# FFN of layer 1: the last 48 rows of up share a weight tile with the last 48 rows of gate

## What is computed

```python
def _ghost_linear(x, idx, lut):
    w = lut[idx]
    return jnp.einsum('bsh,oh->bso', x, w)
gate = _ghost_linear(x, gate_idx, lut)     # gate_idx: 688 x 256
up = _ghost_linear(x, up_idx, lut)         # up_idx:   688 x 256
h = jax.nn.silu(gate) * up
return _ghost_linear(h, down_idx, lut)     # down_idx: 256 x 688
...
h = _layernorm(x, axis=-1) * (1 + cb) + sb
x = x + gb * _L1_ffn_ref(h, ...)
```

## Time and profile before

| what | value |
|---|---|
| median of 3 runs | 1310.63 us (1310.13 to 1314.87) |
| the profiled execution | 1310.77 us |
| its span, first to last instruction | 1309.0 us |
| mean granted TensorE clock | 0.971 of full speed |
| PE busy | 1192.1 us (91%) |
| DVE busy | 935.0 us (71%) |
| ACT busy | 686.7 us (52%) |
| POOL busy | 681.0 us (52%) |
| FFN of layer 1 | 1194.85 to 1309.0, 114 us |

### The profile page before, as it was taken

How to read it: one execution, slowest core, us unless ns; L and a number is a source line. 1 busy time by engine, 2 the same in 40 slices (tenths; PEclk the granted TensorE clock), 3 DMA queues, 4 the chain that set the end, 5 groups by cost and what they waited for, 6 DMA issues and landing times.

```text
span 1309.0 us, 22523 instructions
## 1 busy us (share of the span) xinstructions
PE 1192.1 (91%) x6940; PEld 870.5 (67%) x6940; DVE 935.0 (71%) x2757; ACT 686.7 (52%) x1599; POOL 681.0 (52%) x679
## 2 busy tenths in 40 slices
PE   6888897988569999999999999999999999999998
PEld 5445464545447677686786777867767777667787
DVE  5767787775567786877867868778778687676553
ACT  3356646564354645546546455465465564654432
POOL 0340101011135799998579999857999999000000
PEclk9789999999779999999999999999999999999999
DMA  6431012000124210320420302132022000000000
GB/s 219 132 80 50 26 50 89 26 34 1 65 85 125 76 38 0 135 70 30 139 95 5 129 7 70 49 121 92 26 111 69 2 33 32 0 2 1 17 17 33
DMA packets 36102, 77.93 MB, mean 60 GB/s; under 512 B 8152, under 2 KB 22336, under 8 KB 35248
## 3 DMA queue, kind: packets, MB, share of 16 engines
q1 hardware_dynamic: 26736, 47.13, 10.8%
q0 software_dynamic: 8128, 25.49, 6.0%
q10 hardware_dynamic: 1152, 4.19, 0.8%
HBM read 54.62 MB, written 22.04 MB: 59 GB/s over the span
## 4 chain that ended last, share of the span: by engine, by line
PE 37%; DVE 25%; issue 8%; ACT 3%; DVEq 0%; ACTq 0%
PE bank L1494 10%; PE bank L1468 7%; DVE qk L1093 6%; DVE qkst L1069 5%; PE bank L1479 5%; PE bank L297 5%; PE bank L299 5%; PE bank L298 5%; DVE negmax L1164 2%; DVE probs L1159 2%; DVE x L1149 2%; DVE ytmps L1146 1%; DVE sm L131 1%; DVE sm L129 1%; PE bank L1455 1%
## 5 line engine op out<-in xcount | busy, mean ns | idle before, releaser
L711 POOL TENSOR_SCALAR gtmp<-gidx,lut 128x344 f32<-128x344 int32 (+2 forms) x210 | 299.5, 1426 | 21.3
L1468 PE MATMUL bank<-kT,qT 128*128 128x128 f32 (+3 forms) x512 | 181.7, 444 | 13.2 <-ACT probs L887 13.1
L714 POOL TENSOR_TENSOR gacc<-gacc,gtmp 128x344 f32<-128x344 f32 (+2 forms) x210 | 183.6, 874 | 17.5
L887 ACT ACTIVATE probs<-bank,negmax 128x128 f32<-128x128 f32 (+3 forms) x256 | 135.1, 528 | 60.6 <-DVE negmax L1164 57.0
L297 PE MATMUL bank<-wgH,hL 128*128 128x512 f32 x384 | 155.3, 404 | 1.1 <-issue 1.1
L1164 DVE TENSOR_REDUCE negmax<-bank 128x1 f32<-128x128 f32 (+3 forms) x256 | 122.6, 483 | 42.4 <-PE bank L1469 40.5
L298 PE MATMUL bank<-wgL,hH 128*128 128x512 f32 x384 | 152.3, 397 | 0.0
L299 PE MATMUL bank<-wgH,hH 128*128 128x512 f32 x384 | 152.1, 396 | 0.0
L1494 PE MATMUL bank<-pT,v 128*128 128x512 f32 (+3 forms) x512 | 149.2, 434 | 0.8 <-ACT pT L879 0.7
L1103 DVE TENSOR_REDUCE negmax<-bank 128x1 f32<-128x512 f32 (+3 forms) x176 | 108.1, 636 | 57.4 <-PE bank L1398 57.0
L1069 DVE BATCH_NORM_STATS2 qkst<-qk 128x6 f32<-128x128 f32 x512 | 109.4, 280 | 46.4 <-issue 46.4
(11 more groups left out here) (221 smaller groups left out, 2682.4 us busy)
## 6 DMA issues: line engine op xcount, KB each, us to landing
hH<-h_saved SPq DMA_DIRECT2D x16, 512.0 KB, 4.0
hL<-h_saved SPq DMA_DIRECT2D x16, 512.0 KB, 4.9
qst<-q_parts SPq DMA_DIRECT2D x96, 64.0 KB, 2.4
w_saved<-shi POOLq DMA_DIRECT2D x24, 256.0 KB, 2.3
w_saved<-slo POOLq DMA_DIRECT2D x24, 256.0 KB, 2.6
sraw<-in_wqkv POOLq DMA_DIRECT2D x18, 256.0 KB, 3.0
wgH<-w_saved SPq DMA_DIRECT2D x3, 1536.0 KB, 8.4
wgL<-w_saved SPq DMA_DIRECT2D x3, 1536.0 KB, 11.6
```

The costliest lines, as they stand in the source:

```text
L711: link(pool.tensor_scalar(tmp if j else acc, part, float(j), lut1[0:rows, j:j + 1], ALU.is_equal, ALU.mult))
L714: link(pool.tensor_tensor(acc, acc, tmp, ALU.add))
L1468: pe.matmul(bank[SCORE_BANKS[i % 3]][:, 0:n], qT[:, h, t * P:n], kT[:, h, 0:n], start=True, stop=False)
```

## The change

Gate and up now lie in one row of columns: `wguH` and `wguL` are [128, 2, 11 x 128]. Up's five full tiles come first, then from `GATE0 = 640` on gate's five, and the eleventh tile holds the last 48 rows of gate in its columns 0 to 47 and the last 48 of up in its columns 64 to 111, with zeros between. So the step m = 5 has one product of 6 matmuls in place of two, into `bank[2]`: gate comes out on partitions 0 to 63 and up on 64 to 127. ACT reads the silu's input at partitions 0 to 63 and writes it to `sg` at 64 to 127, DVE multiplies there and writes `hf` at 0 to 63. The following steps of m = 5, `hmH`, `hmL` and the down matmuls, use 64 partitions. Two of POOL's jobs write their result in two pieces, and POOL waits for its own memsets before the first job.

```diff
-        wguH = sb(s1, "wguH", [P, 2, KT, MT * P], F32R)
-        wguL = sb(s1, "wguL", [P, 2, KT, MT * P], F32R)
+        wguH = sb(s1, "wguH", [P, KT, (2 * MT - 1) * P], F32R)
+        wguL = sb(s1, "wguL", [P, KT, (2 * MT - 1) * P], F32R)
...
+            def places(w, k, o):
+                if w == "gate":
+                    return [(slice(0, PIECE), k, GATE0 + o)]
+                if o == 0:
+                    return [(slice(0, PIECE), k, 0)]
+                full = INTER - LAST - o
+                return [(slice(0, full), k, o), (slice(full, PIECE), k, GATE0 + (MT - 1) * P + UP)]
...
+            pool.memset(f32(wguH[:, :, GATE0 + INTER:]), 0.0).then_inc(f_zero, 1)
+            pool.memset(f32(wguL[:, :, GATE0 + INTER:]), 0.0).then_inc(f_zero, 1)
+            pool.wait_ge(f_zero, 2)
             pool.wait_ge(loaded_lut, 16)
...
-                pool.tensor_copy(hi, gacc[:, 0:cols]).then_inc(f_hi, 1)
-                pool.wait_ge(f_hi, i + 1)
-                pool.tensor_tensor(lo, gacc[:, 0:cols], f32(hi), ALU.subtract).then_inc(f_lo, 1)
+                for c, hi, lo in to:
+                    pool.tensor_copy(hi, gacc[:, c]).then_inc(f_hi, 1)
+                pool.wait_ge(f_hi, pieces[i + 1])
+                for c, hi, lo in to:
+                    pool.tensor_tensor(lo, gacc[:, c], f32(hi), ALU.subtract).then_inc(f_lo, 1)
...
-                    act.activation(sg[:, m % 2, :], bank[2 * (m % 2)][:, :], ACT.Silu).then_inc(f_silu, 1)
+                    rows, to = (slice(0, P),) * 2 if m < MT - 1 else (slice(0, UP), slice(UP, P))
+                    act.activation(sg[to, m % 2, :], bank[2 * (m % 2)][rows, :], ACT.Silu).then_inc(f_silu, 1)
                     act.wait_ge(f_h, b * MT + m + 1)
                     act.wait_ge(y2_pe, b * 2)
-                    act.activation(hmH[:, m, :], hf[:, m % 2, :], ACT.Copy).then_inc(f_hhi, 1)
+                    act.activation(hmH[rows, m, :], hf[rows, m % 2, :], ACT.Copy).then_inc(f_hhi, 1)
...
-                    dve.tensor_tensor(hf[:, m % 2, :], bank[2 * (m % 2) + 1][:, :], sg[:, m % 2, :], ALU.mult).then_inc(f_h, 1)
+                    if m < MT - 1:
+                        rows = slice(0, P)
+                        dve.tensor_tensor(hf[:, m % 2, :], bank[2 * (m % 2) + 1][:, :], sg[:, m % 2, :], ALU.mult).then_inc(f_h, 1)
+                    else:
+                        rows = slice(0, UP)
+                        dve.tensor_tensor(hf[rows, m % 2, :], bank[2 * (m % 2)][UP:P, :], sg[UP:P, m % 2, :], ALU.mult).then_inc(f_h, 1)
...
-                    for w in range(2):
+                    for w, first in enumerate((GATE0, 0) if m < MT - 1 else (GATE0,)):
+                        cols = slice(first + m * P, first + (m + 1) * P)
                         for k in range(KT):
-                            last = mm3(pe, bank[2 * (m % 2) + w][:, :], wguH[:, w, k, m * P:(m + 1) * P],
-                                       wguL[:, w, k, m * P:(m + 1) * P], hH[:, k, :], hL[:, k, :], k == 0, k == KT - 1)
+                            last = mm3(pe, bank[2 * (m % 2) + w][:, :], wguH[:, k, cols],
+                                       wguL[:, k, cols], hH[:, k, :], hL[:, k, :], k == 0, k == KT - 1)
...
-                        last = mm3(pe, bank[4 + t // 2][:, (t % 2) * D:(t % 2 + 1) * D], hmH[:, m, rows], hmL[:, m, rows],
-                                   wdH[:, m, :], wdL[:, m, :], m == 0, m == MT - 1)
+                        ks = slice(0, P if m < MT - 1 else UP)
+                        last = mm3(pe, bank[4 + t // 2][:, (t % 2) * D:(t % 2 + 1) * D], hmH[ks, m, rows], hmL[ks, m, rows],
+                                   wdH[ks, m, :], wdL[ks, m, :], m == 0, m == MT - 1)
```

More of the change, by code:

```diff
@@ L42 @@
 LAST = INTER - (MT - 1) * P
+UP = P // 2
 LUT = 16
 PIECE = INTER // 2
+GATE0 = (MT - 1) * P
 NMOD = 6
@@ L682, in _ @@
             pool.dma_start(lut1[:, :], a["lut"].to_broadcast([P, LUT])).then_inc(loaded_lut, 16)
[L684 to L687, removed]
+            def places(w, k, o):
[5 more added lines that the diff above has]
+                return [(slice(0, full), k, o), (slice(full, PIECE), k, GATE0 + (MT - 1) * P + UP)]
+            jobs = [(a[f"idx_{w}"][k * P:(k + 1) * P, o:o + PIECE], P, PIECE,
+                     [(c, wguH[:, kk, to:to + c.stop - c.start], wguL[:, kk, to:to + c.stop - c.start]) for c, kk, to in places(w, k, o)])
+                    for w in ("gate", "up") for k in range(KT) for o in range(0, INTER, PIECE)]
+            jobs += [(a["idx_down"][m * P:min((m + 1) * P, INTER), :], min(P, INTER - m * P), D,
+                      [(slice(0, D), wdH[:, m, :], wdL[:, m, :])]) for m in range(MT)]
+            pieces = [sum(len(job[3]) for job in jobs[:i]) for i in range(len(jobs) + 1)]
             def load_job(i):
-                src, rows, cols, hi, lo = jobs[i]
+                src, rows, cols, _ = jobs[i]
                 pool.dma_start(gidx[0:rows, i % 2, 0:cols], src).then_inc(loaded_idx[i % 2], 16)
@@ L696, in _ @@
             load_job(0)
-            pool.memset(f32(wguH[:, :, :, INTER:]), 0.0).then_inc(f_zero, 1)
-            pool.memset(f32(wguL[:, :, :, INTER:]), 0.0).then_inc(f_zero, 1)
+            pool.memset(f32(wguH[:, :, GATE0 + INTER:]), 0.0).then_inc(f_zero, 1)
+            pool.memset(f32(wguL[:, :, GATE0 + INTER:]), 0.0).then_inc(f_zero, 1)
+            pool.wait_ge(f_zero, 2)
             pool.wait_ge(loaded_lut, 16)
-            for i, (src, rows, cols, hi, lo) in enumerate(jobs):
+            for i, (src, rows, cols, to) in enumerate(jobs):
                 if i in (0, 4, 8):
@@ L706, in _ @@
                 pool.wait_ge(loaded_idx[i % 2], (i // 2 + 1) * 16)
[L707 removed]
+                pool.wait_ge(f_lo, pieces[i])
                 if rows < P:
@@ L1212, in swiglu @@
                     dve.wait_ge(f_hhi, b * MT + m + 1)
-                    dve.tensor_tensor(hmL[:, m, :], hf[:, m % 2, :], f32(hmH[:, m, :]), ALU.subtract).then_inc(f_hlo, 1)
+                    dve.tensor_tensor(hmL[rows, m, :], hf[rows, m % 2, :], f32(hmH[rows, m, :]), ALU.subtract).then_inc(f_hlo, 1)
                 if following is not None:
@@ L1552, in _ @@
             pe.wait_ge(f_zero, 2)
-            pe.wait_ge(f_lo, 2 * 2 * KT + MT)
+            pe.wait_ge(f_lo, 2 * 2 * KT + KT + MT)
             for b in range(NB):
```

## The result

| kernel | median, us | range of its runs | ratio to before |
|---|---|---|---|
| before | 1310.91 | 1310.13 to 1314.87 (4 runs) | 1 |
| after | 1322.78 | 1316.79 to 1324.18 (4 runs) | 1.0073, 95% interval 1.0042 to 1.0105 |

The account below looks back on a forecast made before the run. In batches 0 to 2 the path runs from tile 4 through ACT's scale steps to the transposes, then along PE through the down projection. 1310.8 - 0.8 + 5.2 + 3.5 = 1318.7 us, range 1311.4 to 1321.5.

Parts of the forecast that it names:

- The first thought: PE is the page's busiest engine and loses work, so all the removed matmul time, 5.6 us, would be gained.
- Term 1: Six gate/up matmuls less per batch: nothing gained in batches 0 to 2, -0.8 us once in batch 3.
- Term 2: Down projection with tile 5 on 64 rows: 30 tile-mode switches at 0.17 us, +5.2 us, bounds 0 and +10.5.
- Term 3: Half clock behind the three 2.65 us pauses before the transposes: 2.5 stretches of 1.4 us, +3.5 us, bounds 0 and 4.7.
- B: Rival: no cost for the 64-row tile in the down projection, only the clock; 1313.3 us, chance 0.24.
- C: Rival: the down projection's switches cost but the clock holds behind all three pauses; 1315.2 us, chance 0.06.
- D: Rival: neither switch nor clock costs, the change only fills a wait; 1310.0 us, chance 0.06.
- E: Rival: the transposes wait for something tile 5 sets, so PE's 5.6 us show; 1305.2 us, chance 0.04.
- up to 5.6 us are gained: Sign against term 1: transposes that come earlier in batches 0 to 2 refute it, with this gain.

Follow-up runs that it names:

- e3: The kernel before, all twelve tiles, with only the down matmuls of tile 5 cut to 64 rows; 1318.04 us, ratio to before 1.0038.
- e2: The kernel after with tile 5's hmH, hmL and down matmuls back on 128 rows, gate and up still eleven tiles; 1314.18 us, ratio to before 1.0011.
- e7: The kernel after, tile 5 still on 64 rows, with the scale steps moved early, behind hmH of tiles 2 and 3; 1314.03 us, ratio to before 1.0017.
- e5: e2 with the scale steps moved early, behind hmH of tiles 2 and 3, and DVE's norm parts three per tile; 1308.98 us, ratio to before 0.9966.
- e10: e7 with the 64-row down matmuls of all four token tiles in one row, two mode switches per batch, not eight; 1302.06 us, ratio to before 0.9926.
- e4: e2 with six unused 512-column matmuls put before the transposes of batches 0 to 2; 1311.38 us, ratio to before 0.9991.
- e8: e5 with the down projection reordered: tiles 0 to 4 of token tiles 0 and 2 before their tile 5; 1301.59 us, ratio to before 0.9907.
- e1: The kernel after, unchanged, run again beside before; 1319.57 us, ratio to before 1.0051.

## Why the prediction was right, and where it was off

**What bounds the kernel.** Right. The first thought, a gain of 5.6 us, was dropped because the timeline of ACT in the earlier trace rows has the scale steps start before PE is done with tile 5. The kernel after confirms it: 4.01 and 4.00 us from the silu to the transposes, and a wait that has grown to the 2.65 us that were forecast.

**Term 1, -0.8.** Right in batches 0 to 2 (nothing) and nearly so in batch 3: -0.7. The prediction lets `hf` of tile 5 start at 1294.7 though it has DVE busy until 1294.77, which is most of the missing 0.1. The predicted chain held there: the silu of tile 5 starts 0.66 us behind `hmH` of tile 4 and not 0.54, and the multiply on DVE with its input at partitions 64 to 127 takes 0.69, the same as on 128 partitions, so the 0 to 0.2 put beside it were 0.

**Term 2, +5.2.** Right in kind, and somewhat small: 30 x 0.17 is 5.1, and the stage shows 5.9, 0.39 per pair. Three differences of medians say 5.1 (e3 - before), 5.4 (after - e2) and 5.05 (e7 - e5), and eight switches cost 1.4 us in the stage of e10. The composition held: about 0.09 before the first matmul in the new mode and 0.10 before the second, behind the load that wasn't made ahead, against 0.09 and 0.08 assumed. What was uncertain was whether a row tile behaves like the 96-row matmuls at 150.91 or like the 32-column ones at 151.23. It behaves like the latter. The Trainium skill, TensorEngine Tiling (Array Packing), section Tiling Modes, says that a change of the mode drains TensorE, and lists 64 x 128 as a mode. The traces agree for rows in that each change costs time, 0.17 to 0.20 us in e3 and e10; that the cause is a drain no row shows.

**Term 3, +3.5.** Right in kind, and right in size within what can be told: 2.5 stretches expected, 2 in both traces of after and 3 in that of e2. One costs 1.5 us in after. In e2, against e4, the first costs 1.5 and the second, which begins in the pause, 1.2; 1.4 was assumed. Seven of nine pauses of 2.65 us had the half clock with them; four in five was assumed. e2 - e4, where the only difference is what fills the pause, measures the whole at 2.8 us by the medians and at 4.1 in the stage.

**Sum and range.** The terms as measured, -0.7 + 5.9 + 3.0, make 8.2 where the prediction had 7.9. That it came so close is in part luck: its term 2 is 0.7 too small and its term 3 half a stretch too large. That the first median is 11.9 above before comes from no term: before and after, beside each other again with more runs, are 6.6 apart, and the intervals of the two comparisons, 1.0042 to 1.0105 and 1.0031 to 1.0071, overlap. One kernel's runs lie 8 us apart and more (before: 1309.08 to 1317.33 in 29 runs; e7: 1311.04 to 1320.54 in 10), the slower ones mostly at a lower mean granted clock (in those of before 0.964 in the slowest, 0.972 in the fastest, but also one of 1315.86 at 0.971). That scatter, of which the three runs of before showed 4.7 us, was missing in the range: its upper end was set by the mechanisms alone. Four runs are few for such a spread.

**The rivals.** B (no cost of the 64 rows, 1313.3) is refuted by e3; C (the clock holds, 1315.2) by the two stretches; D by both. E, the gain, is refuted for after, and e8 shows what it would have needed: not one wait less, but two, since behind the transposes' wait stands the one for `hmL` of tile 5.

**What the prediction didn't see** is the size of that second wait. It said that the silu of tile 5 stands behind the scale steps "as before", and went no further, since for the sum it made no difference; and its "up to 5.6 us are gained" for transposes that come earlier leaves the wait out. It mattered for the first repair: the expectation for e5 put the wait for `hmL` of tile 5 at most at about 1 us, it was 1.34 to 1.49 us in all four batches, and with one stretch at half clock besides, which wasn't expected either, e5 came out 3 us slower than expected.

## What to carry to other kernels

Before taking matmuls out of a stream, find the wait that ends last behind them and what releases it: if that is another engine's chain, the matmuls only turn into idle time, and idle time of TensorE can lower its clock. Then look for the next wait in line too; here two had to be covered before 5.4 of 5.6 us appeared. Trimming a matmul from 128 to 64 rows saved nothing here and cost 0.17 to 0.20 us at each change of the tile mode, so pad with zeros to the full array, or put all the small ones one behind the other.

## What the hardware showed beyond that

- Matmuls on 64 rows of 256 columns run 0.12 us apart, as on 128 rows. Only the first behind a change is late, and the one behind it: together 0.17 to 0.20 us.
- Useless matmuls in a pause made the kernel faster: 18 of 512 columns, 2.8 us less by the medians (e4 against e2).
- A pause need not be as long as 2.65 us for the clock to fall. In the FFN of layer 1 there are twelve waits of 1.33 to 1.49 us in the traces of after, e1, e2, e4, e5 and e7; behind two of them 3.4 us ran at granted clock 0.50. These are in e5 (behind the wait that ended at 1293.28) and e7 (behind that which ended at 1240.52):

```profile
1293.28 0.39 PE L299 MATMUL bank<-wdH,hmL 128*128 128x256 f32 x1 [1.49 <-DVE hmL L1234]
```

```profile
1293.76:1297.17 3.41, 3.41 (x19) 3.41 (x18) 0.00 (x0) 0.00 (x0) 0.00 (x0) 0.50 0.00 0
```

```profile
1241.76:1245.17 3.41, 3.41 (x16) 2.96 (x15) 1.26 (x3) 0.36 (x1) 0.00 (x0) 0.50 0.00 0
```

Behind the nine pauses of 1.25 us in before, e3 and e4 there was none. What decides in a single case stays open; no run separated the length of the pause from what runs around it.
